# First layer's value products of a gated cross-attention kernel: full single precision on two column halves instead of high and low parts

## The reference

```python
# first layer, attention
q = (x @ Wq).reshape(B, Nq, h, dh)                 # h = 16, dh = 64
k = (context @ Wk).reshape(B, Nk, h, dh)           # Nk = 154
v = (context @ Wv).reshape(B, Nk, h, dh)
scores = jnp.einsum('bqhd,bkhd->bhqk', q, k) * scale
attn = jax.nn.softmax(scores, axis=-1)
out = jnp.einsum('bhqk,bkhd->bqhd', attn, v).reshape(B, Nq, h * dh)
return out @ Wo + bo
# whole
x = x + tanh(g_xattn[0]) * attention0(layernorm(x), ctx_768, ...)
x = x + tanh(g_ffn[0]) * mixture_of_8_experts(layernorm(x), ...)     # two of eight per row
x = x + tanh(g_xattn[1]) * attention1(layernorm(x), ctx_768, ...)    # 8 heads of 128, all 308 keys
x = x + tanh(g_ffn[1]) * coupling_network(layernorm(x), ...)         # three cycles
```

## Time and profile before

| | |
|---|---|
| three runs, median | 936.27 us (932.23 to 938.24) |
| the profiled execution's own time | 931.24 us |
| its span, first to last instruction | 929.4 us |
| TensorE busy | 880.3 us, 95% of the span |
| VectorE, ScalarE, GpSimd busy | 560.4, 519.2, 367.2 us |
| mean granted TensorE clock | 0.985 |

### The profile page before, as it was taken

One profiled execution on the slowest core, in us unless ns is written; L12 is line 12 of the kernel. 1 busy time (PEld: TensorE's weight loads), 2 busy tenths in 40 slices (PEclk: granted clock), 3 DMA queues, 4 the chain that ended last, 5 costly groups with the idle time before them and its releaser, 6 DMA issues.

```text
span 929.4 us, 20316 instructions
## 1 busy us (share of the span) xinstructions
PE 880.3 (95%) x6813; PEld 799.1 (86%) x6814; DVE 560.4 (60%) x1331; ACT 519.2 (56%) x1466; POOL 367.2 (40%) x530
## 2 busy tenths in 40 slices
PE   6989999999999979999999976999999999999996
PEld 4579999998898759999999976899999999987653
DVE  4666556556655763444434347877777876666456
ACT  6676777677776244344343452756655655652565
POOL 3173444444443224445454541434434443443000
PEclk9999999999999889999999998999999999999998
DMA  9000000420002457777776713000000000000002
GB/s 264 4 1 2 1 1 1 148 69 1 0 1 72 144 204 249 250 242 261 244 262 236 267 42 94 24 23 13 13 23 11 12 1 1 1 2 0 1 0 91
DMA packets 36674, 76.19 MB, mean 82 GB/s; under 512 B 4941, under 2 KB 22721, under 8 KB 36481
## 3 DMA queue, kind: packets, MB, share of 16 engines
q1 hardware_dynamic: 32865, 65.11, 21.3%
q0 software_dynamic: 3744, 10.23, 3.4%
HBM read 66.02 MB, written 9.31 MB: 81 GB/s over the span
## 4 chain that ended last, share of the span: by engine, by line
PE 85%; DVE 6%; DMA 3%; issue 2%; ACT 2%; POOL 1%; SPq 0%; DVEq 0%; POOLq 0%; ACTq 0%
PE banks L535 16%; PE banks L537 15%; PE banks L536 15%; PE banks L1530 14%; PE banks L573 8%; PE banks L563 5%; PE banks L427 2%; PE banks L1809 2%; PE banks L1820 1%; PE banks L1814 1%; PE banks L1802 1%; PE banks L1520 1%; PE banks L542 1%; DMA y_rows<-region_b,home_now 1%; DVE region_b L1404 1%
## 5 line engine op out<-in xcount | busy, mean ns | idle before, releaser
L1084 ACT ACTIVATE region_a<-banks,negmax 128x154 f32<-128x154 f32 (+1 forms) x384 | 161.7, 434 | 29.1 <-DVE negmax L877 28.0
L1530 PE MATMUL banks<-region_b,region_a 128*128 128x128 f32 x1248 | 148.4, 278 | 1.2 <-ACT region_b L1565 1.2
L1530 PEld LDWEIGHTS banks<-region_b,region_a 128*128 128x128 f32 x1248 | 145.4, 195 | 1.8 <-ACT region_b L1565 0.9
L1230 POOL TENSOR_TENSOR region_a<-region_a,recip 128x640 f32<-128x640 f32 x64 | 80.3, 1255 | 137.4 <-DVE recip L881 137.4
L1193 POOL TENSOR_TENSOR region_a<-region_a,recip 128x512 f32<-128x512 f32 x64 | 66.7, 1042 | 138.6 <-DVE recip L881 99.5
L877 DVE TENSOR_REDUCE negmax<-banks 128x4 f32<-128x616 f32 (+1 forms) x128 | 100.4, 785 | 28.3 <-PE banks L563 15.5
L1620 DVE SCALAR_TENSOR_TENSOR region_b<-banks,region_a,region_b 128x128 f32<-128x128 f32 x156 | 43.9, 344 | 104.3 <-PE banks L1530 104.3
L573 PE MATMUL banks<-ident,region_a 128*128 128x128 f32 x640 | 94.5, 279 | 3.9 <-DVE pT_low L887 1.6
L573 PEld LDWEIGHTS banks<-ident,region_a 128*128 128x128 f32 x640 | 72.7, 141 | 14.2 <-issue 9.8
L535 PE MATMUL banks<-xT_high,Wq_high 128*128 128x256 f32 x256 | 77.8, 304 | 3.8 <-DVE q_low L863 2.0
L1066 ACT CAST pT_high<-banks 128x640 fp32r<-128x640 f32 x64 | 44.4, 694 | 65.1 <-PE banks L573 65.1
(11 more groups left out here) (294 smaller groups left out, 2495.0 us busy)
## 6 DMA issues: line engine op xcount, KB each, us to landing
region_a<-in_L_ffn_W SPq DMA_DIRECT2D x39, 1024.0 KB, 5.4
W<-in_L_ffn_W SPq DMA_DIRECT2D x1, 4096.0 KB, 15.9
W<-y_rows SPq DMA_DIRECT2D x16, 256.0 KB, 2.8
out<-x SPq DMA_DIRECT2D x8, 256.0 KB, 2.2
x<-in_x SPq DMA_DIRECT2D x1, 1536.0 KB, 13.7
region_b<-in_L_xattn_Wq SPq DMA_DIRECT2D x1, 1024.0 KB, 9.4
region_b<-in_L_xattn_Wo SPq DMA_DIRECT2D x1, 1024.0 KB, 14.6
xn_rows<-region_b SPq DMA_DIRECT2D x1, 1024.0 KB, 4.8
```

The costliest lines, as they stand in the source:

```text
L1084: e = act.activation(into, source, ACT.Exp, bias=negmax[:, n % 2, u:u + 1], accum_out=sums[:, n % 2, u:u + 1])
L1230: pool.tensor_tensor(probs1[:, n % 2], probs1[:, n % 2], rc, ALU.mult).then_inc(sem("p_norm"), 1)
L1530: mm = pe.matmul(banks[:, 2 * r + part, m * P:(m + 1) * P], W1[r][:, k, cols], xgT[:, r, k, :], start=(k == 0), stop=(k == DK - 1))
```

## The change

The value products of the first layer are issued as `float32`. Each of the two heads of a chunk has its own half of the array's columns and of the output's partitions: the left operand is 64 columns wide, and the matmuls alternate between the halves (first the 128 whole keys, head 0 and head 1, then the keys left over). A call is four matmuls of 256 columns instead of nine. V and the turned probabilities of the first layer are kept once, in single precision: V_high, V_low and p0T_high, p0T_low become V_first, V_second and p0T. ScalarE copies the turned probabilities, VectorE's low part is gone, and TensorE waits for ScalarE's count instead. Of the eight value units ScalarE copies the even ones and VectorE the odd ones. Two zero fills are left of eight. The second layer's products stay as they were.

```diff
+        def values_by(n):
+            return "kv_high" if (n - NC) % 2 == 0 else "kv_sb"
+        def values_count(n):
+            return NC + (n - NC) // 2 + 1
+        def copy_values(copy, n):
+            kind, b, half = kv_units()[n]
+            bank, into = kv_bank(n), V0[b].bitcast(F32)
+            if kind == "v":
+                return copy(whole_values(into, half), bank.rearrange("p (c i n) -> p c i n", c=4, i=2))
+            for j in range(4):
+                last = copy(rest_values(into, half, j), rest_bank(bank, j))
+            return last
...
-                if n >= (4 if n < NC else NC + 3):
-                    pe.wait_ge(sem("kv_sb"), n - (3 if n < NC else 2))
-                    if n < NC:
-                        pe.wait_ge(sem("kv_high"), n - 3)
+                if 4 <= n < NC:
+                    pe.wait_ge(sem("kv_sb"), n - 3)
+                    pe.wait_ge(sem("kv_high"), n - 3)
+                if n >= NC + 3:
+                    pe.wait_ge(sem(values_by(n - 3)), values_count(n - 3))
...
-            p_high, p_low = pT_parts[L.index]
-            for i in range(3):
-                if L is L0:
-                    m = 2 * u + i if i < 2 else 4
-                    cols = slice(64 * i, 64 * i + P) if i < 2 else slice(192, 192 + P)
-                    left = V0[b][0][:, c, cols], V0[b][1][:, c, cols]
-                else:
+            if L is L0:
+                V = V0[b].bitcast(F32)
+                for rest in range(2):
+                    for i in range(2):
+                        m, col = (4, 192 + 64 * i) if rest else (2 * u + i, 128 * i)
+                        mm = pe.matmul(o_ps[64 * i:64 * i + 64, u * PAIR:(u + 1) * PAIR], V[:, c, col:col + 64],
+                                       p0T[:, g % 2, m, :], start=(rest == 0), stop=(rest == 1))
+            else:
+                for i in range(3):
                     m = 3 * u + i if i < 2 else 2
-                    left = V_high[:, c, i, :], V_low[:, c, i, :]
...
+            probs_turned = "pt2_high" if L is L0 else "pt2_low"
...
-                            pe.wait_ge(sem("pt2_low"), s0 + s - 1)
+                            pe.wait_ge(sem(probs_turned), s - 1)
...
             def probsT_rest(n, s):
-                high, low = pT_parts[L.index]
+                if L is L0:
+                    return
...
-                for high, low in V0:
-                    for part in (high, low):
-                        act.copy(part[:, :, 64:128], zero.unsqueeze(2).broadcast_to([P, NC, 64]))
-                        z = act.copy(part[:, :, 192:320], zero.unsqueeze(2).broadcast_to([P, NC, P]))
+                for part in V0:
+                    z = act.copy(part.bitcast(F32)[:, :, 192:320], zero.unsqueeze(2).broadcast_to([P, NC, P]))
```

More of the change, by code:

```diff
@@ L184, in flamingo @@
         ctx_rows = reg_a.part(3 * DC, "p (r d) -> p r d", r=3)
+        reg_a.at = P0_AT
+        p0T = reg_a.part(10 * PAIR, "p (q m n) -> p q m n", q=2, m=5)
         reg_a.at = P0_AT + 20 * PAIR
@@ L452, in dve_kv @@
                     last = dve.tensor_scalar_mul(head_keys(a, 0), keys_of(bank, 0), L.scale)
[L453 to L457, removed]
-                else:
[L459 to L463, removed]
+                elif values_by(n) == "kv_sb":
+                    dve.wait_ge(sem("kv_ps"), n + 1)
+                    dve.wait_ge(sem("v_pads"), 1)
+                    last = copy_values(dve.tensor_copy, n)
+                else:
+                    continue
                 last.then_inc(sem("kv_sb"), 1)
@@ L469, in act_kv @@
                 bank = kv_bank(n)
+                if kind != "k" and values_by(n) != "kv_high":
+                    continue
                 act.wait_ge(sem("kv_ps"), n + 1)
@@ L472, in act_kv @@
                     last = act.activation(head_keys(a, 1), keys_of(bank, 1), ACT.Copy, scale=L.scale)
-                elif kind == "v":
-                    last = act.copy(whole_values(V0[a][0], half), bank.rearrange("p (c i n) -> p c i n", c=4, i=2))
-                else:
-                    for j in range(4):
-                        last = act.copy(rest_values(V0[a][0], half, j), rest_bank(bank, j))
+                else:
+                    last = copy_values(act.copy, n)
                 last.then_inc(sem("kv_high"), 1)
@@ L578, in pe_pair_pv @@
             c = 2 * g + u
[L579 to L585 removed]
+            if L is L0:
[7 more added lines that the diff above has]
+                for i in range(3):
                     m = 3 * u + i if i < 2 else 2
[L587 to L589 removed]
+                    mm = pe_split(pe, o_ps[:, u * PAIR:(u + 1) * PAIR], (V_high[:, c, i, :], V_low[:, c, i, :]),
+                                  (pT_high[:, g % 2, m, :], pT_low[:, g % 2, m, :]), i == 0, i == 2)
             if u == 1:
@@ L646, in transposes @@
                     if first and n == 1 and L is L0:
-                        pe.wait_ge(sem("kv_high"), KV0)
-                        pe.wait_ge(sem("kv_sb"), KV0)
+                        pe.wait_ge(sem("kv_high"), NC + 4)
+                        pe.wait_ge(sem("kv_sb"), NC + 4)
                     if not (first and n == 0):
@@ L883, in probsT_rest @@
             def probsT_rest(n, s):
-                high, low = pT_parts[L.index]
+                if L is L0:
+                    return
                 dve.wait_ge(sem("pt2_high"), s0 + s + 1)
                 at = slice(n % 2 * P, (n % 2 + 1) * P)
-                dve.tensor_tensor(low[:, n // 2 % 2, :, at], probsT_ps[:, 0:640].rearrange("p (m n) -> p m n", m=5),
-                                  high[:, n // 2 % 2, :, at].bitcast(F32), ALU.subtract).then_inc(sem("pt2_low"), 1)
+                dve.tensor_tensor(pT_low[:, n // 2 % 2, :, at], probsT_ps[:, 0:640].rearrange("p (m n) -> p m n", m=5),
+                                  pT_high[:, n // 2 % 2, :, at].bitcast(F32), ALU.subtract).then_inc(sem("pt2_low"), 1)
             def o_rest(g, group):
@@ L1065, in probsT_high @@
                 at = slice(n % 2 * P, (n % 2 + 1) * P)
-                act.copy(pT_parts[L.index][0][:, n // 2 % 2, :, at], probsT_ps[:, 0:640].rearrange("p (m n) -> p m n", m=5))\
+                act.copy((p0T if L is L0 else pT_high)[:, n // 2 % 2, :, at], probsT_ps[:, 0:640].rearrange("p (m n) -> p m n", m=5))\
                     .then_inc(sem("pt2_high"), 1)
```

21 lines of the change are left out of this document (8 added, 13 removed).

## The result

The changed kernel takes **930.54 us**, the median of 20 runs (926.76 to 935.29), against 935.59 for the kernel before on the same chip (20 runs, 931.35 to 940.14). The ratio is **0.9946, 95% interval 0.9930 to 0.9962**. The forecast was 931.3. A second set of runs gave 931.66 (12 runs) and a ratio of 0.9952 (0.9924 to 0.9980). Every ratio in this text is to the kernel before on the same chip. One run of experiment 6 took 1676.05 us at a granted clock of 0.937 and is left out of every figure. So the total came out as forecast; what follows shows that its parts did not all do so, and that over 1 us of it has nothing to do with arithmetic.

What follows compares the result with a forecast made beforehand. TensorE was taken to bound the attention body. Cheaper value calls (3.3 us) and the head (1.7) gave 931.24 - 3.3 - 1.7 = 926.2 us profiled, 931.3 as median; range 926 to 940, 8-in-10 range 922 to 950.

Steps and rivals of the forecast that it cites:

- The bound: First layer's attention body, 63 to 286 us: TensorE busy 222.26 of 223.00 us, so its streaming time is the kernel's time.
- Column halves overlap: Value products: the two column halves run together, so a call streams in 4 rounds of 0.215 us, 0.86 us.
- Rivals 1 and 2: Value products slower: column halves do not overlap, 986 us, chance 0.14; or overlap only in part, 958 us, chance 0.06.
- The form's price: Value calls: 0.09 us entering, 0.14 for slower first record and leaving; call 1.09 us, 0.41 saved per pair, 3.3 in all.
- Rival 3: Value calls: changing form costs little between small forms, so a call nears 0.86 us; 924 us, chance 0.13.
- Costed at nothing: Zero fills, the body's 64 VectorE low parts (52.6 us busy), probability copies and moved waits: no effect on the time.
- rival 4: Body: relieving VectorE brings more than the head, being waited for 0.7 us; counted inside the forecast, no separate chance.
- The head: 26 to 63 us: dropping low parts and dividing value copies saves 1.7 us, between 0 and 3.8.
- 1.3 and 0.2: Head: the maximum at 43.60 comes 1.3 us sooner; the wait at 48.14 for the probabilities' low part gains 0.2.
- holds this stretch and passes on the shift: Later head: GpSimd's normalisation and Wo's low parts set the pace and hand on the earlier start; 1.7 us taken.
- The sum: Whole kernel: 931.24 - 3.3 - 1.7 = 926.2 us profiled; the same saving of 5.0 forecasts a median of 931.3.
- the signs I named as overturning the forecast: Body: TensorE no longer full, or its clock falling to the 1.2 GHz level, which would double what it covers.

Runs made afterwards that it cites:

- experiment 6: Changed kernel with both value calls of a group together in the odd step, for three groups of four; 935.31 us, ratio 1.0009 to the kernel before.
- experiment 4: Changed kernel with three full-precision value matmuls per call over all 128 columns, with zero blocks, instead of four on halves; 944.63 us, ratio 1.0112 to the kernel before.
- experiment 1: Changed kernel with VectorE's unused low part of the turned probabilities, and TensorE's wait for it, put back; 931.25 us, ratio 0.9964 to the kernel before.
- experiment 3: Changed kernel with a call's matmuls ordered half 0, half 0, half 1, half 1, without alternation; 931.92 us, ratio 0.9984 to the kernel before.
- experiment 2: Changed kernel with ScalarE copying every value unit and VectorE subtracting an unread low part, as before; 931.16 us, ratio 0.9968 to the kernel before.
- experiments 5 and 6: Changed kernel with both value calls of a group in one step: even, 937.46 us, ratio 1.0029; odd, three groups of four, 935.31 us, ratio 1.0009.

## Why the prediction was right, and where it was not

**The bound: right.** TensorE is full in the body of both kernels, 1.7 us per pair of whole precision without the halves came out in the time one for one (experiment 4: six pairs 9.4 us longer than before, the last steps 1.6, the head 0.8 shorter; the median 10.0 longer), and the subtractions kept in experiment 1 changed no undisturbed pair.

**Column halves overlap: right.** Rounds of 0.216 us against 0.215 forecast. Rivals 1 and 2 are out, and not by the alternation, which I thought was needed (experiment 3). By the Trainium skill, "TensorE: Matmul & The Clock Gate", Part 3, three column tiles give 2.38 times instead of 3. Two halves here show no such loss.

**The form's price: nearly right.** Entering cost 0.09 as forecast, the slower first round 0.05 as forecast, leaving 0.10 instead of 0.09; a call is 1.015 + 0.09 = 1.105 instead of 1.09. Over eight calls that takes 0.12 from the 0.41 per pair and leaves 0.29; measured are 0.27. The term was 3.3 us and should have been 2.2: I rounded a call's parts to 0.01, and eight calls of 1.1 us subtract almost all of it. A small difference of two large sums needs its terms to a few nanoseconds. Rival 3, cheap changes of form, is out: the price is as in the earlier trace rows.

**Costed at nothing, and wrong:** the low parts of the probabilities in the body. The 0.7 us wait for VectorE's x in the earlier trace rows stood in the text as rival 4. It was the visible part of two waits that lengthened the fifth and sixth pair by 0.5 each (32.73 against 32.22), and it went with the subtractions and came back with them (experiment 1). It is 1.0 us, nearly half as much as the cheaper calls save (eight times 0.27, 2.2 us). The sentence that failed is that in the body what VectorE is relieved of is worth nothing. By luck it makes up for what the call's term lost: six pairs and the last steps save 3.1, where the sum had 0.41 for each, 2.9 for these seven and 3.3 for all eight.

**The head: 0.86 instead of 1.7,** and the 0.86 includes what the calls of the first pair save. The parts that were named, 1.3 and 0.2, add up to 1.5; for the other 0.2 the prediction shows no row. The step that failed is that GpSimd's chain "holds this stretch and passes on the shift". VectorE, by time, in the kernel after:

```profile
40.55 1.19 DVE L420 COPY V_second<-banks 32x128 f32<-32x128 f32 x4 [1.43 <-PE banks L444]
41.77 0.75 DVE L789 BATCH_NORM_STATS2 stats<-x 128x6 f32<-128x256 f32 x2
...
42.72 0.80 DVE L890 TENSOR_REDUCE negmax<-banks 128x4 f32<-128x616 f32 x1
```

Counted from the first value projection the maximum comes at 16.21 us (42.72 - 26.51) against 17.50 (43.60 - 26.10) in the earlier trace rows: 1.3 sooner, just as forecast. But it leads nowhere: next TensorE has its own work back to back until the third transposes. What passed on was a wait of TensorE's that I had not read. The kernel before by time, the first turned probabilities behind the scores of the earlier trace rows:

```profile
42.81 0.74 PE L573 MATMUL banks<-ident,region_a 128*128 128x128 f32 x5 [0.55 <-issue]
```

These transposes wait for the last value unit, whose low part ends at 42.71 in the earlier trace rows; "issue" hides that. After, they start at 42.60, right behind scores that began at 41.87. That is 0.55 us; at the third transposes GpSimd's chain is next late as forecast:

```profile
47.36 0.40 POOL L1207 TENSOR_TENSOR region_a<-region_a,recip 128x128 f32<-128x128 f32 x1
...
47.82 0.77 PE L584 MATMUL banks<-ident,region_a 128*128 128x128 f32 x5 [0.88 <-POOL region_a L1207]
```

0.2 is gained there, by experiment 1 again. 0.6 for the values (experiment 2) and 0.2 for the probabilities are the 0.8 of the head; the little that is left goes to the calls of the first pair.

**The total: right, in part by coincidence.** The sum said 5.0 and 5.05 was measured. Attention gave 3.9, the routing's clock took back 0.3 to 0.9, and the stretch behind the experts gave 1.3 to 2.3, of which a code packet's move is 1.2 to 1.5; neither the sum nor a rival had the last two. That the three add up to the forecast is luck. The last of the signs I named as overturning the forecast, a clock that falls in the body, did not occur; it fell sooner in a stretch that I had not considered.

## What to carry to other kernels

A product whose output is two independent halves of 64 can trade three passes in the reduced type over a half-empty array for four in full precision on column halves, at nearly the same time and without any low parts. Price it start to start, with the change of form in and out: with only eight records per call these changes took 1.9 of the 2.2 us that the streaming saves per pair of tiles (eight times 0.24, of 9.13 - 8 x 0.864). Before merging calls to save changes of form, ask what the emptied steps change into instead and what they wait for: here three or four times 0.15 us won per pair of tiles were outweighed, and the pairs became 0.4 to 1.3 us longer. And where a change is worth a few us in 930, run both kernels with their code shifted as well: a code packet that met a scatter for which GpSimd waits cost TensorE 1.2 to 1.5 us of waiting here.

## What the runs showed of the hardware that I had not expected

- Matmuls on the two column halves overlap fully in both orders of issue that were tried: half 0, 0, 1, 1 took 1.02 us per call, half 0, 1, 0, 1 took 1.01, and the same work in full width 1.39.
- One 16 KB packet of code among the 48 packets of a scatter held back its last three by 1.1 to 1.8 us, and GpSimd's next scatter by 1.6 to 1.9 (4.16, 3.83 and 4.06 against 2.22 us). Ten profiles without such a meeting show none of it.
- Small full-precision matmuls of 128 rows by 8 columns took 0.43 us apiece at the start of the program (32 of them 13.7 us, from 6.26 to 19.93). That is two records of 0.21 us each, what the same form takes in the routing at a granted clock of 0.50 and twice what it takes at 1.00, although the view prints 1.00 at the start.
- From the last query or output product (full array) to the first record of a value product (128x64) it is 0.209 us from start to start, and to the first score (64x128) 0.213, against 0.12 between two query products. Leaving out a step into one small form saved nothing where a step into the other took its place (experiments 5 and 6).
- TensorE's clock fell 12 matmuls sooner in the routing (10.2 us instead of 6.8 at 1.2 GHz) after a change that touched only what ran 10 us and more ahead of it. This is open.
